# Expert layer: the third block of the second product strewn over the ranked chunks, VectorE's rounds written out, the opening gated part later, the scores copied in halves

## What is computed

```python
q = (x_norm @ Wq).reshape(b, t, 2, H, RET // 2)             # H = 4 heads
sim = einsum('btphn,hkpn->pbthk', q, keys)                  # 64 row keys and 64 column keys
sx, ix = top_k(sim, 8)                                      # the best 8 of each
all_sc = sx_rows[..., :, None] + sx_cols[..., None, :]      # 64 sums for each token and head
scores, pk = top_k(all_sc, 8)                               # the best 8 of them
w = einsum('btd,bthkd->bthk', x_norm, down_embed[idx])      # 1024 experts
w = silu(w) * softmax(scores)
experts_states = einsum('bthk,bthkd->btd', w, up_embed[idx])
mlp = silu(x_norm @ Wg + bg) * (x_norm @ Wu + bu) @ Wd + bd # 1024 hidden features
return mlp + experts_states
```

## Time and profile before

| | before |
|---|---|
| median of 3 runs | 2475.89 us (2469.95 to 2478.95) |
| profiled execution | 2467.17 us |
| its span, first to last instruction | 2465.5 us |
| mean granted TensorE clock | 0.987 of full |
| TensorE busy | 2262.2 us (92%) |
| VectorE busy | 1905.2 us (77%) |
| ScalarE busy | 1126.7 us (46%) |
| GpSimd busy | 83.6 us (3%) |

### The profile page before, as it was taken

One profiled execution on the slowest core, in us unless ns is written; L12 is line 12 of the kernel. 1 busy time (PEld: TensorE's weight loads), 2 busy tenths in 40 slices (PEclk: granted clock), 3 DMA queues, 4 the chain that ended last, 5 costly groups with the idle time before them and its releaser, 6 DMA issues. The chain is left out here.

```text
span 2465.5 us, 37808 instructions
## 1 busy us (share of the span) xinstructions
PE 2262.2 (92%) x12582; PEld 1568.6 (64%) x12582; DVE 1905.2 (77%) x5516; ACT 1126.7 (46%) x1542; POOL 83.6 (3%) x135
## 2 busy tenths in 40 slices
PE   5999999899999999999879999898999999999998
PEld 4777778667567567567534444445676675675675
DVE  5768677699899899889844554545898998998997
ACT  1446445454453443443345554553544544434433
POOL 3200000000000000000000000000000000000000
PEclk9999999999999999999989999999999999999999
DMA  7000000000000000000000000000000000000000
GB/s 205 1 1 0 0 0 1 1 1 1 0 0 1 0 0 1 0 0 1 1 1 1 1 1 0 0 1 1 1 9 9 0 9 9 0 9 4 5 9 9
DMA packets 20762, 18.10 MB, mean 7 GB/s; under 512 B 6556, under 2 KB 19872, under 8 KB 20649
## 3 DMA queue, kind: packets, MB, share of 16 engines
q1 hardware_dynamic: 16106, 14.04, 1.9%
q10 hardware_dynamic: 4542, 2.78, 0.4%
HBM read 12.60 MB, written 4.19 MB: 7 GB/s over the span
## 5 line engine op out<-in xcount | busy, mean ns | idle before, releaser
L1380 ACT ACTIVATE f_E<-f_two 128x1024 f32<-128x1024 f32 x256 | 248.3, 1021 | 326.3 <-PE f_two L1265 326.3
L1111 DVE SCALAR_TENSOR_TENSOR f_E<-f_two,f_E 128x1024 f32<-128x1024 f32 x256 | 311.2, 1221 | 90.8 <-ACT f_E L1380 84.4
L1255 PE MATMUL f_acc<-ue,f_mid 128*128 128x256 f32 x1024 | 251.8, 392 | 6.8 <-DVE f_mid L1096 6.8
L1255 PEld LDWEIGHTS f_acc<-ue,f_mid 128*128 128x128 f32 x1024 | 190.1, 192 | 48.1 <-issue 15.4
L1163 PE MATMUL f_two<-f_hT,wg 128*128 128x512 f32 x768 | 210.3, 409 | 0.0
L1350 ACT ACTIVATE f_gate<-f_two,bg 128x512 f32<-128x512 f32 x128 | 88.3, 690 | 257.6 <-PE f_two L1163 257.2
L1163 PE MATMUL f_two<-f_hT,wu 128*128 128x512 f32 x768 | 199.9, 395 | 0.0
L1828 ACT ACTIVATE b_U<-b_two 128x768 f32<-128x768 f32 (+1 forms) x192 | 160.6, 886 | 65.5 <-PE b_two L1698 65.5
L1163 PE MATMUL f_two<-f_hT,deT 128*128 128x512 f32 x768 | 184.3, 395 | 0.0
L1163 PEld LDWEIGHTS f_two<-f_hT,wu 128*128 128x128 f32 x768 | 144.2, 188 | 35.0
L1163 PEld LDWEIGHTS f_two<-f_hT,deT 128*128 128x128 f32 x768 | 144.2, 188 | 35.0
(11 more groups left out here) (262 smaller groups left out, 3973.9 us busy)
## 6 DMA issues: line engine op xcount, KB each, us to landing
x<-in_L_attn_a_x SPq DMA_DIRECT2D x8, 512.0 KB, 7.5
out_x<-x SPq DMA_DIRECT2D x8, 512.0 KB, 2.9
de_rows<-in_L_ffn_down_embed ACTq DMA_DIRECT2D x1, 1024.0 KB, 5.7
wd<-in_L_ffn_Wd SPq DMA_DIRECT2D x1, 1024.0 KB, 9.6
ue<-in_L_ffn_up_embed SPq DMA_DIRECT2D x16, 64.0 KB, 4.9
whole_g<-in_L_ffn_Wg SPq DMA_DIRECT2D x1, 1024.0 KB, 4.9
whole_u<-in_L_ffn_Wu SPq DMA_DIRECT2D x1, 1024.0 KB, 8.6
ffq<-in_L_ffn_Wq ACTq DMA_DIRECT2D x4, 128.0 KB, 8.8
```

The lines of the kernel that those rows point to most:

```text
L1111: dve.scalar_tensor_tensor(out=two_heads, in0=wide(turns, ("R", u))[:], scalar=PICKED_ABOVE, in1=two_heads, op0=ALU.is_gt, op1=ALU.mult).t ...
L1255: mm = pe.matmul(acc[:, j * C:(j + 1) * C], mixed[c % 2][:, j * P:(j + 1) * P], w.ue[:, c, :], start=False, stop=True, skip_group_check=True)
L1380: act.activation(E[:, c % 2, 2 * p:2 * p + 2].rearrange("p h t -> p (h t)"), wide(turns, ("S", u))[:], ACT.Exp).then_inc(S.act_read, 1)
```

## The change

The first three items are on TensorE's and VectorE's order, the others on the opening of the sparse part.

- `AHEAD` goes from 3 to 2. `mlp_out(0)` now stands behind `gates(4)` and `mlp_out(1)` behind `gates(6)`. `mlp_out(2)` leaves the dense part, and its four tiles join the late tiles, 24 in place of 20. `LATE_TILES` has two tiles more in chunk 4 and two more in chunk 7, each time between R(2c) and R(2c+1).
- VectorE's `gated(0)` stands behind `highest(1)` and `half_code(0)` in place of ahead of them.
- VectorE's eight rounds are written out; its loop is gone. Those of the other engines stay.
- All four quarters of the digits are converted by VectorE in one instruction (128x2048); ScalarE's half of it is gone.
- ScalarE copies "s" in two halves of 128x512. TensorE signals quarter 0 (`half_turned`), and ScalarE's first copy signals `opening_scores`. S0 waits for that first copy and for VectorE's conversion, no longer for the whole of "s".

```diff
--- before.py
+++ after.py
@@ -76,13 +76,14 @@
         self.all = [sem(f"{tag}_{n}") for n in (
             "stats_ready mv_ready var_eps rstd_ready shift_step shift_ready xn_ready filled act_read "
             "dve_read sim_half sim_first rank_step below_ready expo_ready total_ready ln_ready digits_ready "
-            "lo_scores shifted heads_added mix_step mix_ready mix_used mid_used x_added "
+            "lo_scores shifted heads_added mix_step mix_ready mix_used mid_used x_added half_turned opening_scores "
         ).split()]
         (self.stats_ready, self.mv_ready, self.var_eps, self.rstd_ready, self.shift_step,
          self.shift_ready, self.xn_ready, self.filled, self.act_read, self.dve_read, self.sim_half,
          self.sim_first, self.rank_step, self.below_ready, self.expo_ready, self.total_ready,
          self.ln_ready, self.digits_ready, self.lo_scores, self.shifted, self.heads_added, self.mix_step,
-         self.mix_ready, self.mix_used, self.mid_used, self.x_added) = self.all
+         self.mix_ready, self.mix_used, self.mid_used, self.x_added, self.half_turned,
+         self.opening_scores) = self.all
 
 
 class AttnSignals:
@@ -821,8 +822,8 @@
         G = TJ * H
         UNITS = 2 * FC
         TURN_X_IN = 4
-        AHEAD = 3
-        LATE_TILES = [(0, 1, 2), (1, 2, 2), (1, 2, 0), (1, 2, 0), (0, 0, 0), (1, 2, 0), (1, 2, 0), (0, 0, 0)]
+        AHEAD = 2
+        LATE_TILES = [(0, 1, 2), (1, 2, 2), (1, 2, 0), (1, 2, 0), (0, 2, 0), (1, 2, 0), (1, 2, 0), (0, 2, 0)]
 
         two, acc = [psum(f"two{n}", 1024) for n in range(3)], psum("acc", TJ * C)
 
@@ -864,7 +865,7 @@
         ROUNDS = B
         RANK_STEPS = 44
 
-        readers = {"x": "both", "m": "act", "r": "act", "g": "both", "d": "both", "s": "act", "z": "dve",
+        readers = {"x": "both", "m": "act", "r": "act", "g": "both", "d": "dve", "s": "act", "z": "dve",
                    "o": "dve", "S": "act", "R": "dve"}
         prepare = [("x", 0), ("m", 0), ("m", 1)]
         dense = [("g", 0), ("r", 0), ("r", 1), ("g", 1), ("r", 2), ("r", 3)] + [("g", f) for f in range(2, FC)]
@@ -984,10 +985,11 @@
                     one_hot(0)
                     if not first:
                         add_x(i - 1)
-                    gated(0)
                     for t in range(1, TJ):
                         highest(t)
                         half_code(t - 1)
+                        if t == 1:
+                            gated(0)
                         places(t)
                         rank_code(t - 1)
                         one_hot(t)
@@ -1075,8 +1077,7 @@
 
                     dve.wait_ge(*turns.filled(i, ("d", 0)))
                     codes = wide(turns, ("d", 0))[:].bitcast(I16).rearrange("p (q t) -> p q t", t=T)
-                    dve.tensor_scalar(digitsT[:, 2:4, :], codes[:, 2:4, :], 1.0 / 2048, None, ALU.mult
-                                      ).then_inc(S.dve_read, 1)
+                    dve.tensor_scalar(digitsT[:], codes, 1.0 / 2048, None, ALU.mult).then_inc(S.dve_read, 1)
                     dve.wait_ge(*turns.filled(i, ("z", 0)))
                     dve.tensor_copy(scoreT[:, 2:4, :].rearrange("p q t -> p (q t)"), wide(turns, ("z", 0))[:]
                                     ).then_inc(S.dve_read, 1)
@@ -1128,10 +1129,8 @@
                     mix(FC - 1)
 
                 rest_of_hT(0, start)
-                a_round(0, steady, first=True, last=False)
-                with dve.Fori(0, (ROUNDS - 2) // 2) as n:
-                    for m in range(2):
-                        a_round(n * 2 + m + 1, steady, first=False, last=False)
+                for i in range(ROUNDS - 1):
+                    a_round(i, steady, first=(i == 0), last=False)
                 a_round(ROUNDS - 1, final, first=False, last=True)
                 add_x(ROUNDS - 1)
 
@@ -1225,9 +1224,8 @@
                         add_bias(pe, w, acc[:, n * 512:(n + 1) * 512], "bd", n, 2)
                     for f in range(2, FC):
                         gates(f)
-                        if f in (3, 4):
-                            mlp_out(f - 3)
-                    mlp_out(AHEAD - 1)
+                        if f in (4, 6):
+                            mlp_out(f // 2 - AHEAD)
 
                     pe.wait_ge(S.digits_ready, i + 1 + START)
                     out = claim(i, turns, ("d", 0))[:].bitcast(BF16)
@@ -1246,6 +1244,8 @@
                         for t in range(TJ):
                             at = q % 2 * T + t * P
                             mm = pe.transpose(out[:, at:at + P], scores[:, q, t].rearrange("p h r -> p (h r)"), w.ident[:])
+                        if q == 0:
+                            mm.then_inc(S.half_turned, 1)
                         if q % 2:
                             mm.then_inc(S.filled, 1)
 
@@ -1267,8 +1267,8 @@
                                            start=True, stop=True)
                         mm.then_inc(S.filled, 1)
 
-                    pe.wait_ge(*turns.act_has_read(i, ("s", 0)))
-                    pe.wait_ge(*turns.act_has_read(i, ("d", 0)))
+                    pe.wait_ge(S.opening_scores, i + 1 + START)
+                    pe.wait_ge(*turns.dve_has_read(i, ("d", 0)))
                     for c in range(FC):
                         if c == FC // 2:
                             pe.wait_ge(*turns.dve_has_read(i, ("z", 0)))
@@ -1365,13 +1365,11 @@
                     gates(7)
 
                     act.activation(idle[:, 1:2], w.eps[:, 0:1], ACT.Exp)
-                    act.wait_ge(*turns.filled(i, ("d", 0)))
-                    codes = wide(turns, ("d", 0))[:].bitcast(I16).rearrange("p (q t) -> p q t", t=T)
-                    act.activation(digitsT[:, 0:2, :], codes[:, 0:2, :], ACT.Copy, scale=1.0 / 2048
-                                   ).then_inc(S.act_read, 1)
+                    opening = wide(turns, ("s", 0))
+                    act.wait_ge(S.half_turned, i + 1 + START)
+                    act.activation(scoreT[:, 0, :], opening[:, 0:T], ACT.Copy).then_inc(S.opening_scores, 1)
                     act.wait_ge(*turns.filled(i, ("s", 0)))
-                    act.activation(scoreT[:, 0:2, :].rearrange("p q t -> p (q t)"), wide(turns, ("s", 0))[:], ACT.Copy
-                                   ).then_inc(S.act_read, 1)
+                    act.activation(scoreT[:, 1, :], opening[:, T:2 * T], ACT.Copy).then_inc(S.act_read, 1)
                     for u in range(UNITS):
                         c, p = u // 2, u % 2
                         act.wait_ge(*turns.filled(i, ("S", u)))
```

## The result

The changed kernel takes 2442.54 us (median of 6 runs, 2432.48 to 2447.75) against 2474.95 (6 runs): ratio 0.9868, 95% interval 0.9840 to 0.9895, so 32 us less. Timed again (experiment 5): 2443.45 against 2475.08, ratio 0.9882 (0.9857 to 0.9908).

What follows compares the result with a forecast made beforehand. A round was taken as TensorE's work (92% busy) plus a few waits. 14 x 1.32 + 1.0 + 1.2 = 20.7 us off the 2475.9 median gave 2455.2 us, range 2443 to 2473.

Steps and rivals of the forecast that it cites:

- S0's chain: Opening of the sparse part: S0 waits for one half copy and VectorE's conversion, so starts 1.32 us earlier a round.
- The third block: TensorE's dense part: 1.72 us gone, only 1.3 us of it counting; its tiles in chunks 4 and 7 cost 0.0.
- Written-out rounds: VectorE's loop turns: 2.42 us idle removed, up to 0.7 us in four rounds not given back; code price taken as 0.
- Last rounds: Last round of each layer: S0 also earlier, but VectorE bounds the tail; gain 1.0 us for f1, 1.2 for f2.
- VectorE at f32's pace: Opening of the sparse part: conversion takes 2.45 us and S0 waits for it; gain 5 us in all, 2471; chance 0.09.
- Stalls of written-out code: VectorE, behind `gated(2)`: one 2.42 us idle in each of 12 rounds, 24 us lost, 2479; chance 0.08.
- Tiles on the path: Chunks 4 and 7, between R fills: moved tiles cost 2.1 to 2.3 us a round where uncovered; 2490; chance 0.07.
- Half the gain: R0 behind the "z" copy or the sequencer ahead of S0: a wait eats half the gain; 2465; chance 0.06.
- second case: Opening of the sparse part: S0 would wait for VectorE's conversion if ScalarE's closeness to PSUM decided; 2471, chance 0.09.
- third rival: VectorE's written-out rounds, fed by the 108 ns compare-and-branch figure: one 2.42 us idle in 12 rounds; 2479, chance 0.08.
- first rival: Opening of the sparse part: VectorE's conversion takes over the wait of S0, gain 0.2 to 0.3 us a round; chance 0.09.
- the second: VectorE's rounds: the written-out code stalls, 24 us lost against 20.7 gained, 2479; chance 0.08.

Runs made afterwards that it cites:

- experiment 5: The changed kernel again, unaltered, timed in five rounds beside the kernel before: 2443.45 us against 2475.08, ratio 0.9882.
- Experiment 1: Kernel before with only the opening of the sparse part changed (all digits converted by VectorE, scores copied in halves, S0's new waits): 2454.02 us, ratio 0.9941.
- experiment 7: Changed kernel with the opening gated part back ahead of the second tile's ranking: 2448.26 us, ratio to the kernel before 0.9892.
- experiment 2: Kernel before with only the third block of the second product strewn over the chunks: 2462.91 us, ratio 0.9976.
- experiments 8: Changed kernel with the four extra tiles in chunks 2 and 3 in place of chunks 4 and 7: 2476.5 us, ratio to the kernel before 1.0011.
- 11: Changed kernel with chunk 4's two extra tiles moved to the end of chunk 3, chunk 7's kept: 2457.29 us (one run).
- 12: Changed kernel with chunk 7's two extra tiles moved to the end of chunk 6, chunk 4's kept: 2452.22 us (one run).
- experiment 4: Kernel before with only VectorE's rounds written out: 2470.84 us, ratio 1.0017.
- experiments 3: Kernel before with only the opening gated part later, VectorE's loop kept: 2469.72 us, ratio 0.9998.
- experiment 6: Changed kernel with VectorE's loop kept (three turns of two rounds): 2444.29 us, ratio to the kernel before 0.9884.
- experiment 10: Changed kernel with ScalarE's seven looped rounds written out too: 2428.06 us, ratio to the kernel before 0.9832.
- experiment 9: Changed kernel with a small silu activation (128x1 column) on ScalarE behind Ln: 2430.37 us, ratio to the kernel before 0.9849.

## Why the prediction was right in its mechanism and wrong in its number

- **S0's chain** (forecast 1.32 us a round): measured 1.43. The parts were right: first copy 41.42 us behind the first gate, as forecast, 0.58 long, VectorE ready just ahead of it. The 0.33 us between copy and S0, carried over from the earlier trace rows, was 0.24: this term was mis-sized. Experiment 1 shows 1.29 of the 1.43 to be the opening's alone; the rest comes with the gated part (experiment 7).
- **The third block** was put at 1.3 to 1.7 us of path. In a steady round at full clock it is worth 0, alone (experiment 2) and behind the opening (experiment 7). What all others add to the opening's 92.93 is 0.26 a round: 0.12 of it is the written-out code and the rest the later gated part. Whether the gated part needs the block for that was not run. My sum didn't count the block, since it went along the chain to S0, but the text let it stand as a gain of its own. The block pays in the last rounds and by the half clock, both below. That the tiles fit chunks 4 and 7 was right; experiments 8, 11 and 12 give the price had they not, 0.86 for two, which I had at 1.06 to 1.13.
- **Written-out rounds**, taken at 0: 0.12 us in each of twelve rounds (experiment 4), 1.4 us in all.
- **Last rounds**, 1.0 and 1.2: measured 2.0 each. ScalarE is straight code there, so silu's table is loaded before g7 is filled. Before, that load came late because Ln's table waited for the silu of g6, at 1176.59:

```profile
1176.59 0.69 ACT L1350 ACTIVATE f_gate<-f_two,bg 128x512 f32<-128x512 f32 x1 [2.11 <-PE f_two L1163]
1177.30 1.28 ACT L1364 ACT_TABLE_LOAD   x1
...
1178.83 1.28 ACT L1350 ACT_TABLE_LOAD   x1
1180.12 0.69 ACT L1350 ACTIVATE f_gate<-f_two,bg 128x512 f32<-128x512 f32 x1
```

  With g6 a block earlier the last silu ends 38.65 us behind the first gate in place of 39.38. The third block alone moves S0 there from 42.78 to 42.04, the opening alone to 42.22, both together (experiment 7) to 40.71; the gated part does nothing there (experiments 3 and 7). I had put g6's lead down as something VectorE can only like, and missed ScalarE.
- **Half clock**, not in the sum at all: this is the step that failed in kind. I read the rows at granted clock 1.00 and the three rounds of 95.1 not at all. The waits of 0.99 and 0.53 us in chunk 4 were to me only room for tiles. Round 6 of f1 before, and behind it the same place in round 2 after the change, where only the second wait is left:

```profile
1111.10 0.39 PE L1265 MATMUL f_two<-f_digitsT,selb 32*128 32x512 bf16 x2 [0.99 <-ACT f_E L1380]
1112.01 1.09 PE L1172 MATMUL f_two<-ident,xn 128*128 128x128 f32 x8 [0.53 <-ACT f_E L1380]
1113.20:1116.60 3.40, 3.40 (x12) 2.27 (x14) 3.29 (x5) 0.96 (x1) 0.00 (x0) 0.50 0.00 0
```

```profile
730.56 1.09 PE L1171 MATMUL f_two<-ident,xn 128*128 128x128 f32 x8 [0.52 <-ACT f_E L1378]
```

- **Sum.** In the profiled executions: 20.7 forecast; + 3.0 in the steady rounds (21.5 in place of 18.5); + 1.8 in the last; + 2.6 half clock in the rounds; + 3.1 elsewhere, chance as far as shown = 31.2. The two behind the forecast are mis-sized terms, 4.8 us; with the half clock in the rounds the mechanism gives 28.1. Off the median that would be 2447.8, inside the range; the last 5 us, which take the result out of it, no run ties to a part of the change. The range's low end was 2443; 16 x 1.6 us off the fastest run, by which it was set, is 2444.4. The medians of after are 2442.5 and, timed again, 2443.45.
- **Rivals.** VectorE at f32's pace: refuted by 1.21 us for 2048. Stalls of written-out code: none in experiment 4. Tiles on the path: not here, and real when placed elsewhere (experiment 8). Half the gain: refuted, since no wait ate any of it; the round fell by 1.55 us where S0 came 1.43 earlier. (Where the prediction speaks of a second case and a third rival, behind its two sentences on the Trainium skill, it means the first rival and the second.) That ScalarE sits closer to PSUM, as the Trainium skill says in "VectorE: DVE Perf Modes", section Specifications, didn't decide: 1.21 us for all digits on VectorE against 1.01 for half of them on ScalarE. The compare-and-branch time that the Trainium skill gives in "Advanced Engine Details and Errata", section Control Flow Timing, doesn't account for the turn of VectorE's loop: it stood 2.43 us idle in experiment 6, and not at all in experiment 4.

## What to carry to other kernels

When the busiest engine stands still once a round, follow the chain that it waits for, and check what a part is worth alone: 1.7 us of TensorE's work ahead of that wait was worth nothing in a steady round, before the wait's own chain was shortened and after. Put left-over work into waits of the busy engine to the tenth of a microsecond; the same four tiles in chunks 2 and 3 cost 1.72 us a round. Look in every stretch of a profile for rounds that differ and for their granted clock before you sum.

## What the runs showed of the hardware

- TensorE falls to half clock (1.2 GHz in place of 2.4) for about 3.4 us in some rounds, and where it does in a steady round, it starts 65 to 67 us behind the first gate, just behind the waits of 0.99 and 0.53 us in chunk 4. In the six profiled kernels with the first of them open (before, experiments 1, 3, 4, 8 and 11): 3, 2, 3, 5, 6 and 7 of 14 rounds. In the eight profiles with two tiles in its place: none of 112. Each costs 0.85 to 1.0 us. The same wait in chunk 7, with chunk 4's filled, brings none (experiment 12). Why it falls in some of these rounds and not in others is not shown.
- The table load of silu goes ahead of ScalarE's wait for g7 in straight code (last rounds, experiment 10) and behind it in the hardware loop, where its 1.28 us are on the path. A small activation of the same function ahead gets 0.54 of it back (experiment 9); then VectorE is the last.
- Each turn of VectorE's loop in the kernel before leaves it idle for 2.3 to 2.6 us. TensorE has no gap where its loop turns; ScalarE waits there for TensorE for 5.66 us, which would hide one. VectorE's written-out code is 0.12 us a round faster (experiment 4); that this is its waits is a guess.
- VectorE converts 16-bit digits out of PSUM at 0.68 us for 1024 and 1.21 for 2048 elements, so by estimate a fixed 0.15 us and twice f32's pace (1.22 us for 1024).
